# The last rows of a two-expert layer: its tiles in two runs, results read back and summed by batch on VectorE, gates by a power on GpSimd

## What is computed

```python
x = x + attention(layernorm(x))
x = x + experts(layernorm(x))
x = x + spectral_and_ffn(layernorm(x))
x = x + experts(layernorm(x))

def experts(x):                                   # 2048 tokens, 8 experts, 128 -> 512 -> 128
    probs = softmax(x @ Wr.T)
    vals, idx = top_k(probs, 2)                   # two experts for a token
    gate = vals / vals.sum(-1)
    return sum over the two: gate_k * (silu(x @ W1[idx_k].T) @ W2[idx_k].T)
```

## Time and profile before

| | us |
|---|---|
| median of 3 runs | 631.68 |
| lowest, highest | 628.78, 633.11 |
| profiled execution, span from first to last instruction | 658.8 |
| first expert layer's last matmul to the first instruction of the next block | 339.09 to 361.70 |
| second expert layer's last matmul to the end of the span | 634.71 to 658.8 |

### The profile page before, as it was taken

The page is one execution under the profiler, slowest core; times in us unless marked ns, Lnnn a source line. Parts: engine busy times, 40 slices in busy tenths (PEclk is TensorE's granted clock), DMA queues, the critical chain, the costliest instruction groups (busy, mean ns, idle before and its releaser), DMA issues. The chain is left out here.

```text
span 658.8 us, 12208 instructions
## 1 busy us (share of the span) xinstructions
PE 513.1 (78%) x3527; PEld 359.1 (54%) x3528; DVE 378.8 (57%) x1248; ACT 250.2 (38%) x518; POOL 318.9 (48%) x373
## 2 busy tenths in 40 slices
PE   2998999999898569569950598999799427689950
PEld 1444555555454259569950344545467327689950
DVE  3879888878968355234434549632947843234423
ACT  1323877676667323134463222101132202234433
POOL 1454479542665554624443953243423755434543
PEclk9999999999998788789995689999999659789995
DMA  6176031233221124234423000000000112222225
GB/s 184 48 215 181 23 102 59 83 112 119 66 65 37 47 83 116 84 84 118 117 85 93 1 0 1 0 0 1 0 1 14 44 57 62 59 77 67 68 66 161
DMA packets 46520, 46.11 MB, mean 70 GB/s; under 512 B 8661, under 2 KB 39952, under 8 KB 46320
## 3 DMA queue, kind: packets, MB, share of 16 engines
q1 hardware_dynamic: 37968, 31.48, 17.3%
q0 software_dynamic: 4544, 9.35, 4.2%
q10 hardware_dynamic: 3952, 4.59, 2.2%
HBM read 31.68 MB, written 15.12 MB: 71 GB/s over the span
## 5 line engine op out<-in xcount | busy, mean ns | idle before, releaser
L1243 ACT ACTIVATE store<-ps 128x512 f32<-128x512 f32 x160 | 90.3, 595 | 48.4 <-PE ps L814 39.9
L1034 DVE TENSOR_REDUCE at_mx<-ps 128x1 f32<-128x512 f32 (+1 forms) x128 | 72.8, 615 | 15.8 <-PE ps L801 15.3
L461 POOL DMA_INDIRECT expert_rows<-r_rows,r_sloti x64 | 62.6, 978 | 31.4 <-issue 18.1
L799 PE MATMUL ps<-at_hats 72*128 72x512 bf16 (+3 forms) x256 | 67.7, 302 | 4.5 <-DVE at_mx L1034 2.7
L597 POOL DMA_INDIRECT expert_results<-store x39 | 37.6, 963 | 51.6 <-issue 19.9
L814 PE MATMUL ps<-at_hats 74*128 74x512 bf16 (+3 forms) x256 | 60.8, 301 | 1.4 <-ACT store L1243 1.1
L1331 POOL TENSOR_SCALAR_AFFINE_SELECT store<-store 128x512 f32<-128x512 f32 x64 | 38.9, 634 | 46.8 <-ACT store L1243 46.8
L597 POOL DMA_INDIRECT expert_results<-at_vall x39 | 37.5, 961 | 49.6 <-DVE at_vall L539 28.1
L831 PE MATMUL ps<-store,at_vext 128*32 128x128 f32 (+3 forms) x512 | 49.2, 461 | 6.7 <-ACT at_oT_more L1211 6.6
L582 PE MATMUL ps<-moe_w,store 128*128 x312 | 45.6, 294 | 7.0 <-ACT store L553 3.6
L582 PE MATMUL ps<-moe_w,at_hats 128*128 x312 | 44.5, 290 | 7.4 <-issue 7.4
(11 more groups left out here) (313 smaller groups left out, 1058.1 us busy)
## 6 DMA issues: line engine op xcount, KB each, us to landing
at_hats<-parts SPq DMA_DIRECT2D x48, 96.0 KB
at_hats<-parts SPq DMA_DIRECT2D x16, 288.0 KB
moe_w<-moe_w_dram SPq DMA_DIRECT2D x8, 512.0 KB, 4.4
store<-ssm_tables_dram SPq DMA_DIRECT2D x35, 86.0 KB
at_vall<-expert_rows SPq DMA_DIRECT2D x39, 64.5 KB
store<-expert_rows SPq DMA_DIRECT2D x39, 64.5 KB
at_hats<-expert_results SPq DMA_DIRECT2D x8, 256.0 KB, 4.8
sm_gates<-expert_results SPq DMA_DIRECT2D x8, 256.0 KB, 5.4
```

What stands on the lines that cost most here:

```text
L461: pool.indirect_dma_start(self.xs_dram[:, :], bass.IndirectOffsetOnAxis(self.sloti[:, n, k:k + 1], 0), self.rows[:, k, n, :], None).then_i ...
L799: pe.matmul(bankA(n)[:, col:col + (t + 1) * P], hatq[0:MROW, slot, h, t * P:(t + 1) * P], hatk[0:MROW, slot, h, 0:(t + 1) * P], start=True ...
L1034: m = dve.tensor_reduce(mx[:, u % 2, t, h:h + 1], bankA(n)[:, 0:(t + 1) * P], AX.X, ALU.max)
L1243: act.activation(pt[:, u % 2, j // 2, S * (j % 2):S * (j % 2 + 1)], bankB(n), ACT.Exp).then_inc(s_e, 1)
```

## The change

**Two runs in the last stage.** The plan of the last stage no longer has one run of tiles for each expert, but two: 16 runs, first for each expert the tiles up to the last row of the first three groups, then for each expert the rest. Every row of the first three groups then lies in tiles 0 to 30 (`SETTLED` = 31 tiles).

**Readback in two parts.** SP waits for the scatters of tiles 0 to 30 and reads back the six blocks of groups 0 to 2, then waits for all and reads the two blocks of group 3.

**Sums on VectorE.** `scale_first` and `add_first` go. `combine(g)` on VectorE does for a group four fused multiply-adds with the first choice, and four with the second. They stand between the last steps of the tile loop. In the second layer ScalarE's queue issues the stores of groups 0 to 2.

**Gates.** exp(gap) is made as a power e**gap on GpSimd, early; VectorE makes the difference (`gaps`) before `slots(3)`, and the gates before step 38. The preparations for the spectral part move into the attention part, beside functions of the same ScalarE table. A drain is added on GpSimd before its first `y` scatters.

```diff
+SETTLED = (2 * (NG - 1) * GT * P + NE * (P - 1)) // P
...
     def plan(self, dve, s):
...
+        n, runs = FIRST[s + 1] - FIRST[s], 2 * NE if last else NE
+        passed = self.passed[:, 0:n * runs].rearrange("p (n r) -> p n r", r=runs)
...
+        if s == STAGES - 2:
+            ch.did(dve.tensor_scalar(ended[:, 0:NE], total, 1.0 / P, all_rows, ALU.mult, ALU.add))
...
+        if last:
+            second = self.second_run[:, 0:n]
+            ch.link(dve.tensor_scalar(second, eid, NE - 0.5, -float(NE), ALU.is_ge, ALU.mult))
+            ch.link(dve.tensor_tensor(eid, eid, second, ALU.add))
...
+    def gaps(self, dve):
+        gap = self.gap
+        self.chain.link(dve.tensor_tensor(gap[:, :], self.top[:, 1, :], self.top[:, 0, :], ALU.subtract))
+        dve.tensor_scalar(gap[:, :], gap[:, :], -87.0, None, ALU.max).then_inc(self.s_gap, 1)
...
-    def gap_exponentials(self, act):
-        act.wait_ge(self.s_gap, 1)
-        act.activation(self.egap[:, :], self.gap[:, :], ACT.Exp).then_inc(self.s_egap, 1)
+    def gap_exponentials(self, pool):
+        pool.wait_ge(self.s_gap, 1)
+        pool.tensor_tensor(self.egap[:, :], self.c["euler"][:, :], self.gap[:, :], ALU.pow).then_inc(self.s_egap, 1)
...
-    def load_results(self, sp):
+    def load_results(self, sp, groups, tiles):
+
         for q in range(4):
-            sp.wait_ge(self.s_st[q], 16 * ((NSLOT - q + 3) // 4))
-        for g in range(NG):
+            sp.wait_ge(self.s_st[q], 16 * ((tiles - q + 3) // 4))
+        for g in groups:
...
+    def combine(self, dve, g):
+
+        for k, done in enumerate((self.s_sum, self.s_out)):
+            dve.wait_ge(self.s_res[k][g], 16)
+            if k:
+                dve.wait_ge(self.s_sum, (g + 1) * GT)
             for t in range(g * GT, (g + 1) * GT):
...
+                dve.scalar_tensor_tensor(self.x[:, t, :], self.ytok[:, k, t, :], self.router.gate[:, k, t:t + 1],
+                                         self.x[:, t, :], ALU.mult, ALU.add).then_inc(done, 1)
...
-            over_slot_tiles(dve, lambda i, u: experts.vector(dve, i, u), begin=11)
+            over_slot_tiles(dve, lambda i, u: experts.vector(dve, i, u), NSLOT - 1, begin=11)
             router.gates(dve)
-            turns.vector_setup(dve)
-            experts.add_second(dve)
+            expert(NSLOT - 1)
+            experts.combine(dve, 0)
+            expert(NSLOT)
+            experts.combine(dve, 1)
+            expert(NSLOT + 1)
+            experts.combine(dve, 2)
+            expert(NSLOT + 2)
+            experts.combine(dve, 3)
...
-            router.gap_exponentials(act)
-            turns.scalar_setup(act)
-            act.wait_ge(router.s_gate, 1)
-            experts.scale_first(act)
+            turns.sines(act)
...
+            pool.drain()
...
+            router.gap_exponentials(pool)
             over_slot_tiles(pool, lambda i, u: experts.results(pool, i, u), NSLOT + 4, begin=13)
-            experts.add_first(pool)
...
-            experts.load_results(sp)
+            experts.load_results(sp, range(NG - 1), SETTLED)
+            experts.load_results(sp, range(NG - 1, NG), NSLOT)
```

More of the change, by code:

```diff
@@ L312, in plan @@
     def plan(self, dve, s):
[L314 to L317, removed]
+        ch, c, begun, ended = self.chain, self.c, self.begun, self.ended
+        at, last, full_rows, all_rows = slice(FIRST[s], FIRST[s + 1]), s == STAGES - 1, -0.49609375, 0.49609375
+        n, runs = FIRST[s + 1] - FIRST[s], 2 * NE if last else NE
+        tiles, change, upto = self.tiles[:, 0:runs], self.change[:, 0:runs], self.tiles_upto[:, 0:runs]
+        passed = self.passed[:, 0:n * runs].rearrange("p (n r) -> p n r", r=runs)
         eid, first_tile, place = self.eid[:, 0:n], self.first_tile[:, 0:n], c["slot_tile"][0:1, 0:n]
@@ L322, in plan @@
             dve.tensor_tensor(self.pad_start[:, :], total, c["region"][0:1, :], ALU.add).then_inc(self.s_pads, 1)
[L324 to L336, removed]
-        ch.link(dve.tensor_tensor(passed_tiles, passed, bc(change[:, :], n, 1), ALU.mult))
+        end = ended[:, NE:2 * NE]
+        if s == STAGES - 2:
+            ch.did(dve.tensor_scalar(ended[:, 0:NE], total, 1.0 / P, all_rows, ALU.mult, ALU.add))
@@ new lines, in plan @@
+        ch.link(dve.tensor_scalar(end, total, 1.0 / P, all_rows if last else full_rows, ALU.mult, ALU.add))
+        ch.link(dve.tensor_scalar(end, end, ROUND, ROUND, ALU.add, ALU.subtract))
+        if last:
+            end = ended[:, :]
+        ch.did(dve.tensor_tensor(change, end, begun[:, 1:runs + 1], ALU.subtract))
+        ch.link(dve.tensor_tensor(tiles, end, begun[:, 0:runs], ALU.subtract))
+        ch.link(dve.tensor_tensor_scan(upto, c["one"][0:1, 0:runs], tiles, 0.0, ALU.mult, ALU.add))
@@ L1101, in _ @@
             for u in range(UNITS):
+                if u == 3:
+                    turns.importance(dve)
                 for j in range(NA):
@@ L1135, in _ @@
             router.second_choice(dve, 3)
+            router.gaps(dve)
             expert(7)
@@ L1909, in _ @@
             router.plan(dve, 2)
-            over_slot_tiles(dve, lambda i, u: experts.vector(dve, i, u), begin=3)
+            over_slot_tiles(dve, lambda i, u: experts.vector(dve, i, u), NSLOT - 1, begin=3)
             router.gates(dve)
-            experts.add_second(dve)
+            expert(NSLOT - 1)
+            experts.combine(dve, 0)
+            expert(NSLOT)
+            experts.combine(dve, 1)
+            expert(NSLOT + 1)
+            experts.combine(dve, 2)
+            expert(NSLOT + 2)
+            experts.combine(dve, 3)
         @block.sync
@@ L1932, in _ @@
             sp.wait_ge(s_x2, B)
-            experts.load_results(sp)
-            experts.store(sp, out)
+            experts.load_results(sp, range(NG - 1), SETTLED)
+            experts.load_results(sp, range(NG - 1, NG), NSLOT)
+            experts.store(sp, NG - 1, out)
+            sp.wait_ge(experts.s_stored, 16 * NG)
         @block.gpsimd
@@ L2093, in _ @@
             over_slot_tiles(act, lambda i, u: experts.scalar(act, i, u))
-            router.gap_exponentials(act)
-            act.wait_ge(router.s_gate, 1)
-            experts.scale_first(act)
+            for g in range(NG - 1):
+                experts.store(act, g, out)
         @block.tensor
```

90 lines of the change are left out of this document (44 added, 46 removed).

## The result

| | before | after |
|---|---|---|
| median of the runs of the comparison | 632.39 us (4 runs, 628.78 to 633.4) | 611.31 us (4 runs, 611.03 to 620.68) |
| span of the profiled execution | 658.8 us | 609.3 us |
| mean granted clock of TensorE in it | 0.893 | 0.935 |

The ratio leaves out the run of 620.7 us, the slow one of the four; such runs come back in experiment 6.

A forecast was written before the change was run, and what follows sets the result against it. Scatter and readback latency and serial sums across three engines were taken to bound both layer ends; gains of 4.5 + 5.0 less plan costs of 2.1 and 0.6 gave 6.8 us, so 624.9 from 631.68 us, range 619 to 631.5.

The forecast's parts named there:

- terms 1 to 5: Layer ends: VectorE sums at 0.285 us, earlier readback, last `y` 3.5 us later; gains of 4.5 and 5.0 us.
- The 18.6 us of the second end: Second layer's end before the change: time counted from TensorE's last product to VectorE's last sum, with TensorE idle.
- The late readback: Rival, 6%: VectorE waits in the sums for blocks, delaying the last tiles; at the slow end 641 us.
- sums beside scatters: Rival, 11%: three scatter issues beside the sums each hold them 0.96 us, 5.8 us in all; 630.7 us.
- The barrier behind it (5.67 us) is unchanged: First layer's end: the stretch from last sum to next block was taken to stay at 5.67 us.
- term 5: Second layer's end: last sum at 648.3 instead of 653.34, gain 5.0 us; the 5.5 us behind it stay.
- term 1: Cost of a sum on VectorE: 0.285 us for all 32 in a layer, once GpSimd's adds are gone.
- Term 6: Longer plans ahead of the tile loops: last plan 1.3 us longer; charged 2.1 us in first layer, 0.6 in second.
- The rival of cheaper plans: Rival, 12%: pauses of the tile loop hide the longer plans' cost; 622.2 us, down to 619.
- A loop that differs by more than 3 us: Sign of being wrong: the tile loop, not its end, differs by more than 3 us in a layer.
- a pause of 4.50 us: Rival, 8%: tile-loop pauses of 3 to 4.5 us without visible cause may come or go; 620.9 or 628.9 us.

The follow-up runs named there:

- experiment 6: The changed kernel run again, unchanged, as a control: median 613.9 us of 6 runs, 610.99 to 620.8.
- experiment 1: The kernel before, unchanged, profiled a second time: 630.0 us, span 628.3 us.
- experiment 7: The changed kernel with the sums of groups 1 and 2 moved behind the last tile's `y`: 610.5 us, ratio 0.970 to the kernel before.
- experiment 5: The kernel before with a GpSimd drain right behind its last scatter of `y` in either expert layer, ahead of its adds: 621.4 us, ratio 0.988.
- experiment 9: The changed kernel with GpSimd, behind its last scatter, made to wait without work for VectorE's last sum: 621.7 us, ratio 0.986 to the kernel before.
- experiment 2: The kernel before with only the change's two GpSimd drains added: 623.6 us, ratio 0.990.
- experiment 8: The changed kernel with one instruction of the last plan carried out seven times instead of once: 623.6 us, ratio 0.990 to the kernel before.
- experiment 3: The changed kernel without its two GpSimd drains: 619.2 us over 4 runs, ratio 0.980 to the kernel before.

## Why the prediction was wrong in its size

**Right: terms 1 to 5 as far as the last sum, the two ends.** Sums at 0.296 us (0.285 forecast), the last `y` 3.4 us later (3.5), from last product to last sum 12.3 and 12.2 us (12.5 and 13.6). The 18.6 us of the second end were counted from 634.71, the end of the last tile but one (the table of the profile before has the same time); the last product ends at 635.72, so it is 17.6 in that trace, 17.0 in the other. The gain of both ends is 9.6 to 10.0 us against 9.5. The late readback did not come: VectorE waited for none of the six blocks.

**Right: sums beside scatters.** Beside an issue eight sums took 2.37 us and without one 2.38, so in the changed kernel no scatter's issue held a sum; it is GpSimd's issue that is 0.1 us longer there. Three issues fell beside sums in a layer, as the rival had it. Beside GpSimd's adds 16 sums took 7.41 us in experiment 1, 0.46 each, the longest 1.42; in experiment 7, which has no adds, 16 took 4.66 us, 0.29 each, and the longest of the layer's 32 was 0.352. That the adds made the difference fits these rows; how they would do it no row shows.

**The step that failed: "The barrier behind it (5.67 us) is unchanged"**, and its twin in term 5, that the store and what follows take the 5.5 us they take now. The prediction took a stretch with no busy engine for a constant. Experiments 5 and 9 show from both sides what it is. Counting from GpSimd's last instruction to the next block: 344.45 to 351.85 in the kernel before, profiled again, 7.4 us; with the early drain (experiment 2) 343.82 to 349.25, 5.4 us; in experiment 9, held until 340.79, 5.6 us. Since its last drain GpSimd had issued 71 indirect transfers in the first (32 of rows, 39 of `y`) and 47 in the other two (8 and 39). Estimated from these rows, it is about 0.08 us for each transfer and 1.5 us of barrier: 1.5 + 71 x 0.083 = 7.4 and 1.5 + 47 x 0.083 = 5.4. The second layer, counted to the end of the span, has the same 71 and 47, and 7.2 us (before) and 5.4 us (experiment 9, from the end of its wait); and the drain of some 6 us behind 71 transfers in experiment 5 fits the 5.9 of the sum. That it goes by the number of transfers rests on these two numbers, 71 and 47; what GpSimd does in that time no row shows. In the kernel before, the adds pushed this behind them, and 5.7 of the 7.4 us stood open behind VectorE's last sum. The change takes the adds away, GpSimd is done at 332.8, and what it finishes is over while VectorE waits for the last group. That is 4.1 + 1.7 = 5.8 us, which the prediction had in front of it: term 1 says that "ScalarE's and GpSimd's instructions go and nothing else waits for them", and the barrier did wait for GpSimd.

**Term 6, the plans, was right, and was thought to be missing.** The last plan lasts 4.24 us (511.26 to 515.50) instead of 2.87 (523.88 to 526.75): 1.37 more, 1.3 forecast. In the second layer TensorE's pitch there grew by 1.2 us, and router and loop are 1.0 longer; 0.6 was forecast. In the first layer, where the prediction charged 2.1 in all, the 1.37 us are taken as paid; the loop's own difference cannot show it. The rival of cheaper plans falls by experiment 8, and the first loop's -3.9 is no proof for it, for the next reason.

**Not in the prediction: the granted clock.** Of the same kernel, 6 runs of 10 are at 611.0 to 611.6 and a clock of 0.932 to 0.935, the others at 616 to 621 and 0.914 to 0.922. The kernel before had 0.898 to 0.924 in the 48 runs beside the experiments. But the mean clock of a run cannot be compared between the two kernels, since it counts the ends, in which TensorE does nothing and the clock is lower, 0.55 to 0.66 in these executions. By stretch it was:

| stretch | before, again | after | without drains (experiment 3) |
|---|---|---|---|
| to the end of attention | 0.98 | 0.97 | 0.97 |
| first tile loop | 0.93 | 0.98 | 0.93 |
| last product to next block | 0.55 | 0.66 | 0.60 |
| spectral part | 0.94 | 0.95 | 0.92 |
| second router and tile loop | 0.88 | 0.88 | 0.85 |
| last product to the end | 0.55 | 0.65 | 0.59 |

Weighted by their lengths, the four stretches in which TensorE works stand at 0.94, 0.95 and 0.93. So most of the way from 0.916 to 0.935 is idle time that is shorter, and not work at a higher clock. The lines for the first loop and the end behind it, of the kernel before and of the changed one (columns as in experiment 8):

```profile
226.50:329.10 102.60, 87.57 (x709) 84.49 (x707) 47.44 (x234) 38.77 (x84) 52.31 (x55) 0.93 0.40 105
329.10:351.80 22.70, 0.01 (x1) 0.00 (x0) 9.49 (x26) 10.18 (x28) 7.04 (x6) 0.55 0.37 99
```

```profile
228.70:327.40 98.70, 82.90 (x709) 80.19 (x708) 52.61 (x255) 38.88 (x87) 55.38 (x56) 0.98 0.47 125
327.40:341.20 13.80, 0.00 (x0) 0.00 (x0) 5.87 (x25) 0.05 (x1) 2.50 (x3) 0.66 0.17 53
```

What the clock does to work is seen in windows of 10 us from the start of the spectral part; the changed kernel:

```profile
341.00:351.00 10.00, 3.96 (x10) 2.09 (x10) 8.05 (x44) 0.78 (x1) 7.54 (x12) 0.50 0.01 2
351.00:361.00 10.00, 8.38 (x28) 4.14 (x28) 3.60 (x12) 3.85 (x10) 10.00 (x13) 0.94 0.00 0
361.00:371.00 10.00, 9.88 (x37) 5.07 (x37) 5.29 (x12) 4.16 (x13) 7.38 (x8) 1.00 0.00 0
```

and without drains (experiment 3, the slowest of its four runs):

```profile
345.00:355.00 10.00, 3.66 (x9) 1.99 (x9) 7.92 (x44) 0.78 (x1) 7.24 (x12) 0.50 0.01 3
355.00:365.00 10.00, 8.38 (x21) 4.34 (x21) 2.75 (x11) 3.85 (x10) 8.05 (x10) 0.67 0.00 0
365.00:375.00 10.00, 9.88 (x29) 4.18 (x27) 3.22 (x8) 2.48 (x10) 5.20 (x8) 0.82 0.00 0
```

Both begin at 0.50, behind the idle end of the layer. In the second window the one is at 0.94 and does 28 matmuls, the other at 0.67 does 21, with TensorE busy for 8.38 us in both. The spectral part took 138.1 us in the one and 143.9 in the other. Of the 11.5 us between these two executions 5.8 lie there, 3.6 in the first loop, 1.4 in the second and 0.8 in attention. Both profiled executions of the changed kernel are near 611 (span 609.3), so that its own higher runs lose their 5 to 10 us at the same places is likely and not shown.

**The account.** Ends -9.6, block ends -5.8, plans about +2.3 (the first layer's 1.37 of length and the 1.0 of the second) give -13.1. The two profiled executions differ by 19.0; the other 5.8 stand in stretches that the change leaves alone, most of it in the first loop, which ran at 0.98 against 0.93. A loop that differs by more than 3 us was one of the prediction's own signs of being wrong, and this one does, by 3.9. That the clock makes all of these 5.8 us is argued from these rows and not shown. The medians differ by 21, since the kernel before is at 632.4 in that comparison and at 630 where it was profiled again. Against its four higher runs the changed kernel gains 9 to 14 us on 630, about what the rows say; in the six others it gains 18 to 19. Why more than half of its runs are of this kind is open. From the last product to the next block it is now 13.8 us instead of 22.7 in the first layer, which would speak for the change itself; but the kernel without drains has the same 13.7 and was near 611 in 2 runs of 10. Of the rivals, none happened: sums were not blocked, the readback was not late, the plans were not hidden, and a pause of 4.50 us as in the earlier trace rows that came or went is not what made the difference; the size came from two things that stood in no rival.

## What to carry to other kernels

An empty stretch behind the last work of a block is not a constant: ask which engine's last instruction comes late, and what that engine still has to finish, here GpSimd, 7.4 us after 71 indirect transfers. What helped was to give it nothing to do at the end, or to put a drain where it waits anyway: 5.67 us behind the last sum became 1.53 either way. Work overlapped with the last tiles must not stand ahead of the last tile's own output: put it into the wait that follows (9.8 us from last product to last sum in experiment 7, instead of 12.3). Before pricing a change of 1%, have more than one profiled execution of the kernel: here it was 27 us off, and runs of one kernel lay 10 us apart. Do not take the mean granted clock of a run for the clock of its work where idle stretches differ (0.935 against 0.916 here, with 0.95 and 0.94 in the stretches that work): read it by stretch.

## What the runs showed of the hardware

- After 71 indirect transfers GpSimd held the end of a block for 7.4 us behind its last instruction and the end of the program for 7.2 (experiment 1), after 47 for 5.4 to 5.6 us (experiments 2 and 9); a drain in idle time removed it, leaving 1.53 us behind the last sum (experiment 5). The drain itself lasted some 6 us behind 71 transfers, estimated from the 5.98 us between the scatter's issue and the add behind the drain.
- A power on GpSimd on 16 elements a partition took 2.93 us in the changed kernel (L403), as estimated from those on 4 and 8.
- Issuing a scatter took 1.06 to 1.09 us beside VectorE's three-input sums in the changed kernel, 0.96 without; in experiment 7 one beside them took 1.09 and the next 0.96. Eight sums took 2.37 us beside an issue, 2.38 without.
- TensorE's granted clock was 0.55 over idle ends of 22.7 us (experiment 1), 0.65 to 0.66 over ends of 16.0 and 13.8 us in the changed kernel, and 0.59 to 0.60 over ends of 16.0 and 13.7 us in experiment 3. Behind a pause of 8.5 us the next tile ran at 0.65 with a pitch of 2.9 us instead of 1.9 (experiment 8); behind one of 3.1 us the clock was 1.00 and the pitch 1.9 (changed kernel).
